# A four-layer kernel: the probabilities' lower halves made one step later, directly behind the next step's maximum, with the small jobs, the value scales and the buffers moved to match

## What is computed

```python
x = x + L0_xattn(layernorm(x), ctx)        # attention on the keys themselves
x = x + L0_ffn(layernorm(x))               # 32 experts, top 4, two sizes of expert
x = x + L1_xattn(layernorm(x), ctx)        # grouped attention, below
x = x + L1_ffn(layernorm(x))               # quantized feed-forward, ternary weights

def L1_xattn(h, enc):                      # 16 query heads, 4 key heads, head size 128
    q = rms_norm((h @ Wq).reshape(B, S, 16, 128), q_norm_w)
    k = rms_norm((enc @ Wk).reshape(B, 1601, 4, 128), k_norm_w)
    v = (enc @ Wv).reshape(B, 1601, 4, 128)
    ...
    probs = softmax(q k^T / sqrt(128)); out = probs v
    return out.reshape(B, S, 2048) @ Wo
```

## Time and profile before

| | |
|---|---|
| Median of 3 runs | 1729.36 us (1729.26 to 1730.32) |
| The profiled execution: own time | 1723.86 us |
| The profiled execution: span | 1721.9 us |
| Mean granted TensorE clock | 0.909 |
| TensorE, VectorE, ScalarE, GpSimd busy | 76%, 73%, 58%, 32% of the span |

### The profile page before, as it was taken

The page is one execution under the profiler, slowest core; times in us unless marked ns, Lnnn a source line. Parts: engine busy times, 40 slices in busy tenths (PEclk is TensorE's granted clock), DMA queues, the critical chain, the costliest instruction groups (busy, mean ns, idle before and its releaser), DMA issues. The chain is left out here.

```text
span 1721.9 us, 24069 instructions
## 1 busy us (share of the span) xinstructions
PE 1315.6 (76%) x8423; PEld 1151.6 (67%) x8423; DVE 1265.1 (73%) x2252; ACT 1004.1 (58%) x1834; POOL 557.8 (32%) x419
## 2 busy tenths in 40 slices
PE   6898488888468688688878868887886879787645
PEld 5797277777357677577767757776775768676523
DVE  4666688887577877678778767877876787786457
ACT  4674277887355565556655655665665566565335
POOL 2342254432543322423223242322333332131034
PEclk9999599999789998899989889999998999998868
DMA  6141489996187565556566546665674556555510
GB/s 203 63 164 55 146 269 305 294 317 219 44 154 144 106 143 112 110 105 116 110 122 141 105 100 118 112 124 108 135 129 94 110 111 126 106 100 112 111 50 25
DMA packets 499696, 228.99 MB, mean 133 GB/s; under 512 B 441236, under 2 KB 479256, under 8 KB 499192
## 3 DMA queue, kind: packets, MB, share of 16 engines
q1 hardware_dynamic: 495016, 214.99, 54.2%
q0 software_dynamic: 4560, 12.46, 2.8%
HBM read 106.41 MB, written 11.93 MB: 69 GB/s over the span
## 5 line engine op out<-in xcount | busy, mean ns | idle before, releaser
L2066 DVE SCALAR_TENSOR_TENSOR ga_halves<-ga_probs,ga_inv_sum,ga_halves 128x1024 f16<-128x1024 f32 (+1 forms) x256 | 356.5, 1433 | 164.8 <-ACT ga_halves L1906 164.8
L1898 ACT ACTIVATE ga_probs<-ga_ps_s,ga_neg_max 128x1200 f32<-128x1200 f32 (+1 forms) x256 | 235.6, 926 | 368.8 <-DVE ga_neg_max L2051 368.8
L1906 ACT ACTIVATE ga_halves<-ga_probs,ga_inv_sum 128x1024 f16<-128x1024 f32 (+1 forms) x256 | 233.2, 958 | 83.2 <-DVE ga_inv_sum L2059 81.7
L1789 POOL TENSOR_TENSOR ga_oT<-ga_out_n,ga_oT 128x256 fp32r<-128x256 f32 x64 | 59.5, 930 | 499.0 <-ACT ga_oT L1922 499.0
L2093 PE MATMUL ga_ps_t<-side_w_kv,side_encT 128*128 128x256 f32 (+1 forms) x1170 | 165.9, 295 | 71.0 <-POOL side_encT L1755 37.6
L2093 PE MATMUL ga_ps_s<-side_kT,ga_qT 128*128 128x400 f32 (+1 forms) x768 | 176.9, 384 | 45.8 <-DVE side_kT L2026 24.4
L2046 DVE TENSOR_REDUCE ga_part_max<-ga_ps_s 128x1 f32<-128x1200 f32 x128 | 178.9, 1398 | 39.3 <-PE ga_ps_s L2093 39.1
L2093 PEld LDWEIGHTS ga_ps_t<-side_w_kv,side_encT 128*128 128x128 f32 (+1 forms) x1170 | 149.4, 192 | 79.3 <-issue 39.2
L2093 PE MATMUL ga_ps_s<-ga_kT,ga_qT 128*128 128x400 f32 (+1 forms) x768 | 169.2, 371 | 43.0 <-ACT ga_probs L1898 26.2
L2093 PEld LDWEIGHTS ga_ps_s<-side_kT,ga_qT 128*128 128x128 f32 x768 | 155.8, 213 | 53.8 <-DVE side_kT L2026 26.7
L2093 PEld LDWEIGHTS ga_ps_s<-ga_kT,ga_qT 128*128 128x128 f32 x768 | 147.4, 203 | 52.6 <-ACT ga_probs L1898 30.3
(11 more groups left out here) (294 smaller groups left out, 2509.3 us busy)
## 6 DMA issues: line engine op xcount, KB each, us to landing
ex_raw<-in_L_ffn_packed SPq DMA_DIRECT2D x63, 704.0 KB
side_w_q_raw<-in_L_xattn_Wq SPq DMA_DIRECT2D x16, 512.0 KB
side_w_q_raw<-in_L_xattn_Wo SPq DMA_DIRECT2D x16, 512.0 KB, 4.5
mix_y_rows<-ex_y SPq DMA_DIRECT2D x63, 128.0 KB
side_enc<-in_ctx_turned SPq DMA_DIRECT2D x12, 512.0 KB, 4.9
ca_keys<-in_ctx_turned SPq DMA_DIRECT2D x12, 464.0 KB, 5.9
ca_cache<-in_ctx SPq DMA_DIRECT2D x4, 1024.0 KB, 7.0
ga_pT<-ga_halves SPq DMA_TRANSPOSE x256
```

The source lines that it names most:

```text
L1789: nc.gpsimd.tensor_tensor(oT[:, h, LO, :], out_n[:, :], f32(oT[:, h, HI, :]), ALU.subtract).then_inc(out_lo, 1)
L1898: nc.scalar.activation(dst, src, ACT.Exp, bias=neg_max[:, n % 2:n % 2 + 1], accum_out=half_sum[:, n % 4, k:k + 1]).then_inc(exped, 1)
L1906: nc.scalar.activation(halves[n % 2][:, HI, a:z], probs[n % PB][:, a:z], ACT.Copy, scale=inv_sum[:, n % 2:n % 2 + 1]).then_inc(high, 1)
L2066: nc.vector.scalar_tensor_tensor(halves[n % 2][:, LO, a:z], probs[n % PB][:, a:z], inv_sum[:, n % 2:n % 2 + 1], halves[n % 2][:, HI, a:z], ...
```

## The change

In `grouped_attention`:

- VectorE's order in a step becomes: maximum of n, lower halves of n - 1, small jobs of n - 1, inverse of n. It is the same in s0.
- SyncE transposes the lower halves of n - 1 and then the high halves of n. `weigh`, `take_values`, `split_result` and GpSimd's `result_low` come one step later, and the drain has one step more.
- The small jobs of a group stand one to two steps earlier, so that s7 prepares nothing for the next group and s0 and s1 hold a `q` and a `kv` job each. `qT` is cut by pairs of heads instead of tiles of tokens; its second half is made in s0 of the group that uses it. `norm` and `xT` move from s0 and s2 to s6 and s7, and the first two encoder pieces from s0 and s1 of the next group to s6 and s7.
- `v` has three buffers instead of two, `qT` one instead of two.

In `experts`: the bound on the values is worked out in the first seven blocks instead of ahead of the first; the operations are the same, and TensorE and GpSimd no longer wait for the bound before the first block.

```diff
@@ experts: scalar, vector, tensor, gpsimd
+                if i == WEIGHTS_SQUARED:
+                    act.wait_ge(side.norm_in, 48)
+                    nc.scalar.activation(value_w[:, :, :], value_w[:, :, :], ACT.Square).then_inc(act_routed, 1)
...
+                if i == LARGEST_OF:
+                    largest_values()
+                if i == BOUND_ROOT - 1:
+                    value_bound()
+                if i == SCALED:
+                    value_scales()
...
-            pe.wait_ge(dve_routed, BOUND)
+            pe.wait_ge(dve_routed, TOKENS)
...
+                if i == WEIGHTS_SQUARED + 1:
+                    value_weights_summed()
+                if i == SPREAD:
+                    largest_spread()
@@ grouped_attention
-    DRAIN = 4
+    DRAIN = 5
...
-        u, half = ((n - 3) // 2, 0) if n % 2 else (n // 2 - 2, 1)
+        u, half = n // 2 - 2, n % 2
...
-                0: [("q", 0, to)],
-                1: [("q", 1, to), ("q_eps", 0, to)],
-                2: [("kv", 0, to), ("kv", 1, to)],
-                3: [("kv", 2, to), ("kv", 3, to), ("k_eps", 0, to)],
-                4: [("kv", 4, to), ("kv", 5, to)],
-                5: [("kv", 6, to), ("k_eps", 1, to), ("qT", 0, to), ("qT", 1, to)],
-                6: [("kT", 0, to), ("kT", 1, to)],
-                7: [("kT", 2, to), ("kT", 3, to)]}[s]
+                0: [("qT", 1, g), ("q", 0, to), ("kv", 0, to)],
+                1: [("q", 1, to), ("kv", 1, to), ("q_eps", 0, to)],
+                2: [("kv", 2, to), ("kv", 3, to), ("k_eps", 0, to)],
+                3: [("kv", 4, to), ("kv", 5, to)],
+                4: [("kv", 6, to), ("k_eps", 1, to), ("qT", 0, to)],
+                5: [("kT", 0, to), ("kT", 1, to)],
+                6: [("kT", 2, to), ("kT", 3, to)],
+                7: []}[s]
...
-            if s == 0:
+            if s in (6, 7):
+                jobs = [("enc", s - 6, row)] + jobs
+            if s == 6:
                 jobs = jobs + [("norm", 0, row)]
-            if s == 2:
-                jobs = [("xT", 0, row)] + jobs
+            if s == 7:
+                jobs = jobs + [("xT", 0, row)]
         row, at = divmod(g + 1, G)
-        if at == 0 and row < B and s < 4:
-            jobs = jobs + [("enc", (0, 1, 3, 2)[s], row)]
+        if at == 0 and 0 < row < B and s < 2:
+            jobs = [("enc", (3, 2)[s], row)] + jobs
...
-        qT = [sb(f"qT{i}", [P, 2, HG, S], F32R) for i in range(2)]
+        qT = sb("qT", [P, 2, HG, S], F32R)
...
-        v = [side.v, sb("v1", [P, 2, KT, DH], F16)]
+        v = [side.v] + [sb(f"v{i}", [P, 2, KT, DH], F16) for i in (1, 2)]
...
@@ sync
+                if 0 <= n - 1 < N:
+                    turn_probs(n - 1, LO, low)
                 if n < N:
                     turn_probs(n, HI, high)
-                    turn_probs(n, LO, low)
...
@@ vector
-                first_of_group = n % STEPS == 0
-                if n < N and not first_of_group:
+                if n < N:
                     largest(n)
+                if 0 <= n - 1 < N:
+                    probs_low(n - 1)
                 if n:
                     for e in plan[n - 1]:
                         entry(e)
-                if n < N and first_of_group:
-                    largest(n)
                 if n < N:
                     invert(n)
-                    probs_low(n)
```

More of the change, by code:

```diff
@@ L906, in experts @@
     LAST_PIECE = 5
+    WEIGHTS_SQUARED, LARGEST_OF, SPREAD, BOUND_ROOT, SCALED = 0, 2, 3, 5, 6
     SPLITS_AFTER = 2
@@ L1113, in _ @@
                     gather(i + AHEAD)
+                if i == BOUND_ROOT:
+                    pool.wait_ge(dve_routed, BOUND)
+                    nc.gpsimd.tensor_tensor(root[:, :], bound[:, :], half_power[:, 0:1], ALU.pow).then_inc(pool_ready, 1)
                 if i - 1 in KEYS_SUMMED:
@@ L1816, in _ @@
                 g, s = n // STEPS, n % STEPS
-                if n % 2 and 0 <= (n - 5) // 2 < UNITS:
-                    result_low((n - 5) // 2)
+                if n % 2 == 0 and 0 <= n // 2 - 3 < UNITS:
+                    result_low(n // 2 - 3)
                 for e in plan[n]:
@@ L1935, in _ @@
                     probs_high(n)
-                if n % 2 == 0 and 0 <= n // 2 - 2 < UNITS:
-                    take_values(n // 2 - 2)
                 if n % 2 and 0 <= (n - 5) // 2 < UNITS:
-                    split_result((n - 5) // 2)
+                    take_values((n - 5) // 2)
+                if n % 2 == 0 and 0 <= n // 2 - 3 < UNITS:
+                    split_result(n // 2 - 3)
                 for e in plan[n]:
@@ L2128, in ring @@
                     pe.wait_ge(q_normed, g + 1)
-                    for h in range(HG):
-                        mm = nc.tensor.transpose(out[:, h * P:(h + 1) * P], qn[:, m, h * DH:(h + 1) * DH], eye[:, :])
+                    for i in range(HG):
+                        h, t = 2 * m + i // QT, i % QT
+                        mm = nc.tensor.transpose(out[:, i * P:(i + 1) * P], qn[:, t, h * DH:(h + 1) * DH], eye[:, :])
                 elif kind == "kT":
@@ L2147, in score @@
                 h, t, p = s // QT, s % QT, g % 2
-                if s == 0:
-                    pe.wait_ge(*emptied(("qT", QT - 1, g)))
+                if s in (0, STEPS // 2):
+                    pe.wait_ge(*emptied(("qT", 2 * s // STEPS, g)))
                 for k in range(NB):
```

88 lines of the change are left out of this document (45 added, 43 removed).

## The result

The changed kernel takes 1670.44 us (median of 3 runs, 1663.83 to 1674.21) against 1729.36 us: 0.965 of the time before, 95% interval 0.960 to 0.970. The profiled execution took 1670.44 us, span 1668.5. A second set of five runs gave 0.968 (0.966 to 0.969).

The account below looks back on a forecast made before the run. The kernel was taken as a loop of waits with no engine full. Plain groups 14.7, pairs 10.5, groups 0 and 1 12, group 15 14, experts 3, drain -1 sum to 53: 1729.4 - 53 = 1676 us, range 1636 to 1714.

Parts of the forecast that it names:

- plain groups 4 5 8 9 12 13 14: Seven groups away from the ends of token rows: each 71.1 us before, 69.0 forecast, 2.1 gained each, 14.7 in all.
- group 15: Last group, with hardly any small jobs: steps fall from about 7.9 to 5.4 to 5.9 us, 49 against 63.0, gain 14.
- Light steps: Steps without a small job: the next maximum waits only for the scores, not the lower halves; 5.4 us instead of 7.7.
- s1: Second step of a plain group: exponentials start at 6.7 us instead of 2.1, so the step takes 10.0.
- the squares' wait: ScalarE's kv job waits until VectorE has summed the squares of q; counted as 1.3 us in s1, 1.2 in s2.
- the bank chain: TensorE fills a bank only once VectorE has emptied it, and scores queue behind; alone 8.7 us in s1, 8.2 in s2.
- The clock: TensorE's half clock, costing more now that TensorE is in the chain: 0.6 us added to a plain group.
- Collisions: Lower halves give way to GpSimd's earlier-started splits of w_out in s3 and w_in in s6: 2.4 us a plain group.
- The lock decides: Rival: lower halves' collisions with GpSimd stay at 5.5 us a group, plain groups 71.5, total 1709 us; chance 0.16.
- Slower by the squares' wait in full: Rival: whole wait in s1 and s2 comes on top, 6.1 us longer in each of 14 groups, 1761 us; chance 0.12.
- Pairs: Two groups around a token row's end: TensorE's 11.33 us stand goes, 13 us added; 154.5 becomes 151, 10.5 gained in all.
- Experts: First block starts up to 7.9 us earlier, less the gathering of first tokens; between 0 and 7.9, taken as 3 gained.

## Why the forecast held, point by point

The ledger of the profiled executions, from the starts of the maxima (us gained):

```
                                       forecast   measured
group 0                                  11         10.6
group 1                                   1         -0.7
plain groups 4 5 8 9 12 13 14            14.7       10.6
pairs 2+3, 6+7, 10+11                    10.5       21.4
group 15                                 14         13.4
behind the last maximum                  -1          1.3
up to the first maximum                   3         -3.2
sum                                      53         53.4
```

The forecast was 1676 us, the median measured is 1670.44: by the medians the gain is 59 us, by the two profiled executions 53.4. That the sum of the ledger agrees to 1 us is luck. The pairs gained 11 us more than forecast and the end 2 more; against that the start is 6 us short of its forecast, the plain groups 4 and group 1 2.

- *Light steps* (5.4 forecast, 5.47 measured) and so groups 0 and 15: right, mechanism and size.
- *s1.* The forecast of 10.0 rested on the squares' wait, with "Without that wait the bank chain would give 8.7". The 8.7 failed: two products, `q` and `kv`, stand behind the bank of `qT`, which is free 4.7 us behind the maximum, and 8.7 has room for one. The chain measured 9.43 by itself and 9.84 with the squares' wait at the granted clock 1.00, and 11.0 at 0.84. So the wait was worth 0.4 us in s1 and not 1.3, and in most groups nothing. In s2 the forecast held (9.22 against 9.4, 8.06 against 8.2 without the wait).
- *The clock.* 0.6 us a group was too little: it costs 1.1 in s1 and 0.9 in s4 of group 9, and 1.5 more in s7 of two of the seven plain groups.
- *Collisions.* I had placed them in s3 (`w_out`) and s6 (`w_in`), each as a coin's toss, 2.4 us together. In the changed kernel neither falls there. The one that does is in s4, for ScalarE's hand-over is not what releases `w_out`: its place in GpSimd's queue behind the key scale is. It costs 2.0 us a group without the clock, so the term was near in size and wrong in place. The rule of the Trainium skill that the prediction set beside it (SBUF — State Buffer, "Who interferes with whom") says that whoever issues first holds the shared port for its whole instruction. The rows agree: the second lower-half instruction waits out `w_out` when it comes behind it, and GpSimd waits when it is the other way round (2.96 us for 2.37).
- *"The lock decides"* named the right mechanism for the largest single loss, but not its extent: in a plain group the lower halves met GpSimd for more than 0.2 us in one step of eight, and over the kernel they took 307.8 us, 2.4 a step against 2.79 before.
- *Slower by the squares' wait in full:* refuted by taking the wait away: s1 moved by 0.4 us at most, s2 by 1.2.
- *Pairs.* The term was too small by half. The 11.33 us stand of TensorE went, and of the 13 us that I set against it for `norm`, `xT` and the encoder splits about 9 are there: a pair takes 147.4 on average, two plain groups 138.5. With the lower halves in their own step a pair takes 144, 2 more than two plain groups. So the gain owes nothing to the later lower halves; they cost 3 us a pair.
- *Experts.* Forecast +3, measured 0 within 2: the gathering of the first tokens takes all that the earlier start gives. The prediction named this cover and then took 3 from bounds of 0 to 7.9; the lower bound would have been right. The 3.2 us lost in the ledger are within what this start varies by.
- *The inverse last.* I had worked out the price of late jobs and of the late inverse as part of each step's length, and never asked what the same lower halves would cost in another place. The change gains 57 us and its order gives away 153 more: it spares the light steps 0.9 us each, and puts 2 us in front of the jobs, of the inverse and of all that follows from them.
